# Two chained cross-attention layers on one core: every third late layer-1 step multiplies fp32 probabilities as they are, and one unit's heads are scaled in three blocks

## What is computed

```
text, ip = ctx[:, :77], ctx[:, 77:]          # 77 and 947 tokens
q, k, v      = heads(x @ Wq.T), heads(text @ Wk.T),    heads(text @ Wv.T)
k_ip, v_ip   = heads(ip @ Wk_ip.T), heads(ip @ Wv_ip.T)
out_text = softmax(q k^T / 4) v              # 20 heads, over 77 tokens
out_ip   = softmax(q k_ip^T / 4) v_ip        # over 947 tokens
x = x + (out_text + out_ip) @ Wo.T + bo
```

## Time and profile before

| | us |
|---|---|
| runs | 3522.02, 3520.13, 3520.0 |
| median | 3520.13 |
| span of the profiled execution, first to last instruction | 3517.6 |
| TensorE busy in it | 3406.7 (97%) |
| VectorE, ScalarE, GpSimd busy | 2044.4, 1845.3, 1095.2 |

### The profile page before, as it was taken

The page is one execution under the profiler, slowest core; times in us unless marked ns, Lnnn a source line. Parts: engine busy times, 40 slices in busy tenths (PEclk is TensorE's granted clock), DMA queues, the critical chain, the costliest instruction groups (busy, mean ns, idle before and its releaser), DMA issues.

```text
span 3517.6 us, 65886 instructions
## 1 busy us (share of the span) xinstructions
PE 3406.7 (97%) x24832; PEld 2900.3 (82%) x24832; DVE 2044.4 (58%) x5565; ACT 1845.3 (52%) x4030; POOL 1095.2 (31%) x932
## 2 busy tenths in 40 slices
PE   6999999999999999999999999999999999999978
PEld 4888978887888888888888878888788888889755
DVE  4444445556555565665656556656566656565678
ACT  2333333556454555555655555555555556565757
POOL 2111010234332332233333232333423322222467
PEclk8999999999999999999999999999999999999989
DMA  5433822233348333233356423324335532222233
GB/s 183 107 77 64 104 82 74 70 88 83 82 83 76 93 75 83 76 100 84 94 76 71 97 71 76 80 74 107 86 74 78 69 61 62 55 55 53 52 78 64
DMA packets 659087, 282.78 MB, mean 80 GB/s; under 512 B 481010, under 2 KB 609730, under 8 KB 658772
## 3 DMA queue, kind: packets, MB, share of 16 engines
q1 hardware_dynamic: 658772, 278.57, 38.2%
HBM read 199.44 MB, written 79.04 MB: 79 GB/s over the span
## 4 chain that ended last, share of the span: by engine, by line
PE 88%; DVE 6%; ACT 2%; issue 1%; POOL 1%; SPq 1%; DMA 1%; POOLq 0%; DVEq 0%; ACTq 0%
PE acc L1095 9%; PE acc L1088 9%; PE acc L1090 8%; PE acc L1091 8%; PE acc L1096 8%; PE acc L1089 7%; PE score L1055 4%; PE score L1139 4%; PE spare L1139 4%; PE score L1057 3%; PE av L1126 3%; PE av L1130 3%; PE score L1176 2%; PE spare L1176 2%; PE score L1225 2%; PE spare L1225 2%
## 5 line engine op out<-in xcount | busy, mean ns | idle before, releaser
L1298 ACT ACTIVATE prob<-score 128x512 f32<-128x512 f32 x1219 | 729.3, 598 | 1252.5 <-PE score L1057 1244.4
L1698 POOL TENSOR_TENSOR prob_lo<-prob,prob_hi 128x512 fp32r<-128x512 f32 x624 | 816.1, 1312 | 1525.5 <-ACT prob_hi L1301 1524.9
L1088 PE MATMUL acc<-tok_v,prob_hi 128*128 128x300 f32 x2240 | 904.1, 404 | 0.9 <-issue 0.9
L1090 PE MATMUL acc<-tok_lo,prob_hi 128*128 128x256 f32 (+1 forms) x2560 | 755.5, 295 | 0.0
L1095 PE MATMUL acc<-tok_v,prob_lo 128*128 128x278 f32 (+1 forms) x2560 | 745.8, 291 | 0.0
L1301 ACT ACTIVATE prob_hi<-score 128x512 fp32r<-128x512 f32 x1219 | 726.0, 596 | 0.0
L1091 PE MATMUL acc<-tok_lo,prob_hi 128*128 128x256 f32 (+1 forms) x2560 | 719.5, 281 | 0.0
L1096 PE MATMUL acc<-tok_v,prob_lo 128*128 128x256 f32 (+1 forms) x2560 | 717.7, 280 | 0.0
L1089 PE MATMUL acc<-tok_v,prob_hi 128*128 128x256 f32 x2240 | 627.4, 280 | 0.0
L1090 PEld LDWEIGHTS acc<-tok_lo,prob_hi 128*128 128x128 f32 (+1 forms) x2560 | 484.2, 189 | 9.1 <-issue 7.2
L1091 PEld LDWEIGHTS acc<-tok_lo,prob_hi 128*128 128x128 f32 (+1 forms) x2560 | 483.6, 189 | 6.3 <-issue 1.0
(11 more groups left out here) (325 smaller groups left out, 5141.1 us busy)
## 6 DMA issues: line engine op xcount, KB each, us to landing
k_ring<-k_scr SPq DMA_DIRECT2D x160, 384.0 KB
tok_v<-v_scr SPq DMA_DIRECT2D x158, 176.0 KB, 3.3
v_ring<-v_scr SPq DMA_DIRECT2D x160, 148.5 KB, 3.4
ctx_t<-in_ctxT SPq DMA_DIRECT2D x16, 1024.0 KB, 9.1
q_ring<-q_scr SPq DMA_DIRECT2D x160, 96.0 KB
v_scr<-v_stage SPq DMA_DIRECT2D x32, 440.0 KB, 2.6
v_scr<-v_stage SPq DMA_DIRECT2D x36, 330.0 KB, 9.6
tok_stage<-in_ctx SPq DMA_DIRECT2D x32, 256.0 KB, 2.9
```

The costliest lines, as they stand in the source:

```text
L1088: e.matmul(out_a[:, 0:SEG + VCOLS], p_hi, tok_v[0:kk, c, seg, v_lo:v_lo + SEG + VCOLS], start=first, stop=False)
L1090: e.matmul(out_a[:, t0:t0 + SEG], p_hi, tok_lo[0:kk, c, seg * SEG:(seg + 1) * SEG], start=False, stop=False)
L1298: e.activation(prob[:, es, :], bank_s[:, :], ACT.Exp, scale=SCALE)
L1698: e.tensor_tensor(prob_lo[:, ps, :], prob[:, es, :], prob_hi.bitcast(F32)[:, ps, :], ALU.subtract).then_inc(s_low[1], 1)
```

## The change

1. In the tail every third step is *whole* (`whole`, WHOLE_EVERY = 3: steps 1, 4, 7, ... of the 125). A whole step has one exp, into `prob`, no subtraction, and two products of `v_ring`, read as plain fp32, with `prob` itself. Its exp makes the next use of its slot wait for its products instead of for its subtraction.
2. The other tail steps have their subtraction on GpSimd, all of them.
3. The heads of unit 14 are scaled in three blocks of 8, 8 and 4, both parts in place in `heads_out`, each block when its heads are there; after the last, two sums (`combine_sum`) of text and image halves write `attn`.

```diff
+BY_BLOCKS = (LAST - 1, LAST)
+WHOLE_EVERY = 3
...
+        if u in BY_BLOCKS:
+            put_off(*[("combine_block", u, NM - 1, i) for i in range(3)], *[("combine_sum", u, st) for st in range(ST)])
+        else:
+            put_off(*[("combine", u, i) for i in range(3 if layer == 0 else 7)])
...
+        if u in BY_BLOCKS and h + 1 in [end for _, end in BLOCKS[:-1]]:
+            m = [end for _, end in BLOCKS].index(h + 1)
+            if u == LAST:
+                urgent.append((n + 5, lambda: last_block(m)))
+            else:
+                urgent.append((n + 5, lambda: put_off(*[("combine_block", u, m, i) for i in range(3)])))
...
-    on_pool = [layer_of[n] == 1 and (n < tail or n % 8 != 4) for n in range(len(chunks))]
+    on_pool = [layer_of[n] == 1 for n in range(len(chunks))]
+    whole = [n >= tail and (n - tail) % WHOLE_EVERY == 1 for n in range(len(chunks))]
...
@@ TensorE, av1
+                    if whole[n]:
+                        for k in range(UNIT_KEYS):
+                            mm = e.matmul(both[0:n_out[k], 0:SQ], weights[k].bitcast(F32), prob[:, n % E_SLOTS, queries[k]],
+                                          start=r == 0 and k == 0, stop=r == 0 and k == 0 or r == NU - 1 and k == 1,
+                                          skip_group_check=r > 0 or k > 0)
+                        mm.then_inc(s_main, 1)
+                        continue
...
@@ ScalarE, score
-                        e.wait_ge(s_low[on_pool[m]], low_nth[m])
+                        if whole[m]:
+                            e.wait_ge(s_main, m + 1)
+                        else:
+                            e.wait_ge(s_low[on_pool[m]], low_nth[m])
+                    if whole[n]:
+                        e.activation(prob[:, es, :], bank_s[:, :], ACT.Exp, scale=SCALE).then_inc(s_exp, 1)
+                        continue
...
@@ VectorE, combine_block piece 1, and combine_sum
-                        e.tensor_tensor(at, ho[:, :, :, 0:DH], wide[0], ALU.mult).then_inc(s_comb, 1)
+                        text = ho[:, :, :, 0:DH]
+                        e.tensor_tensor(at if u == LAST else text, text, wide[0], ALU.mult).then_inc(s_comb, 1)
...
+                elif kind == "combine_sum":
+                    _, u, st = s
+                    ho = heads_out[1][:, st, :, :]
+                    e.wait_ge(s_comb, comb_base[u, NM - 1] + 4)
+                    e.tensor_tensor(attn[:, st, :, :], ho[:, :, 0:DH], ho[:, :, DH:2 * DH], ALU.add).then_inc(s_comb, 1)
```

More of the change, by code:

```diff
@@ L508, in unit_done @@
             return
-        put_off(*[("combine", u, i) for i in range(3 if layer == 0 else 7)])
+        if u in BY_BLOCKS:
+            put_off(*[("combine_block", u, NM - 1, i) for i in range(3)], *[("combine_sum", u, st) for st in range(ST)])
+        else:
+            put_off(*[("combine", u, i) for i in range(3 if layer == 0 else 7)])
         if layer == 0:
@@ L600, in rows_of @@
         urgent.append((n + 3, lambda: turn_head(u, h)))
-        if u == LAST and h + 1 in [end for _, end in BLOCKS[:-1]]:
-            urgent.append((n + 5, lambda: last_block([end for _, end in BLOCKS].index(h + 1))))
+        if u in BY_BLOCKS and h + 1 in [end for _, end in BLOCKS[:-1]]:
[4 more added lines that the diff above has]
+                urgent.append((n + 5, lambda: put_off(*[("combine_block", u, m, i) for i in range(3)])))
         if h == HEADS - 1:
@@ L739, in cross_attention_pair @@
     layer_of = [UNITS[u][0] for _, u, _, _ in chunks]
-    on_pool = [layer_of[n] == 1 and (n < tail or n % 8 != 4) for n in range(len(chunks))]
+    on_pool = [layer_of[n] == 1 for n in range(len(chunks))]
+    whole = [n >= tail and (n - tail) % WHOLE_EVERY == 1 for n in range(len(chunks))]
     low_nth, seen = [], [0, 0]
     for n in range(len(chunks)):
-        seen[on_pool[n]] += 1
+        seen[on_pool[n]] += not whole[n]
         low_nth.append(seen[on_pool[n]])
@@ L921, in cross_attention_pair @@
         close0 = {s[1]: i for i, s in enumerate([s for s in o.steps if s[0] == "fuse_root"])}
-        comb_base, comb_here, base = {}, {}, 0
+        comb_base, comb_done, comb_here, base = {}, {}, {}, 0
         for s in o.steps:
@@ L929, in cross_attention_pair @@
             elif s[0] == "combine_block":
-                comb_base.setdefault(s[1], base)
+                comb_base.setdefault(s[1:3], base)
                 base += 2 if s[3] == 0 else 1
+                comb_done[s[1:3]] = base
+            elif s[0] == "combine_sum":
+                base += 1
+                comb_done[s[1], NM - 1] = base
         ip_nth = {s[1]: i for i, s in enumerate([s for s in o.steps if s[0] == "ip_norm"])}
@@ L1249, in _ @@
                     if k == 0:
-                        e.wait_ge(s_comb, comb_base[u] + (5 * (m + 1) if u == LAST else COMBINED[layer]))
+                        e.wait_ge(s_comb, comb_done[u, m if u == LAST else NM - 1] if u in BY_BLOCKS else comb_base[u] + COMBINED[layer])
                         if layer == 0:
@@ L1398, in _ @@
                     n = s[1]
-                    if not on_pool[n]:
+                    if not on_pool[n] and not whole[n]:
                         ps, es = n % P_SLOTS, n % E_SLOTS
@@ L1595, in _ @@
                     h0, h1 = BLOCKS[m]
-                    i0 = comb_base[u] + 5 * m
+                    i0 = comb_base[u, m]
                     ho = heads_out[1][:, :, h0:h1, :]
@@ L1694, in _ @@
                     n = s[1]
-                    if on_pool[n]:
+                    if on_pool[n] and not whole[n]:
                         ps, es = n % P_SLOTS, n % E_SLOTS
@@ L1875, in _ @@
                     w, nth_close = MW[m], close_nth[u]
-                    e.wait_ge(s_comb, comb_base[u] + (5 if u == LAST else COMBINED[layer]))
+                    e.wait_ge(s_comb, comb_done[u, 0 if u == LAST else NM - 1] if u in BY_BLOCKS else comb_base[u] + COMBINED[layer])
                     if nth_close:
```

## The result

The changed kernel takes 3509.51 us (median of 8 runs, 3506.83 to 3514.22) against 3520.07 us for the kernel before (8 runs, 3516.76 to 3525.22): a ratio of 0.9969, 95% interval 0.9959 to 0.9979. That is 10.6 us less, 0.31%, where 7.1 us less was forecast; the range of the prediction holds it, and of its three cases (faster by over 0.2%, within, slower) the first came. The profiled execution took 3506.83 us; it is the fastest of the eight.

A forecast was written before the change was run, and what follows sets the result against it. In 3440 to 3479 us GpSimd was taken as longest, with little between it and the other engines. By stretch, -4.2, -0.6 and -2.3 sum to -7.1 us against the median of 3520.13: 3513.0 us, range 3504 to 3524.

The forecast's parts named there:

- the price: Each whole step: two plain fp32 products instead of four fp32r ones cost TensorE +0.395 us at full clock.
- the blocks: Unit 14's heads, scaled earlier in three blocks, leave less VectorE work at its end: -3.0 us, gain of 1.3 to 4.5.
- three signs of being wrong: Exps waiting over some 3 us on products, fp32 products above 0.9 us a step, or TensorE's gap after unit 14 unchanged.
- The gap: TensorE's wait after unit 14's last head was to be 1 to 3.7 us instead of 5.17.
- 3308 to 3430 us, -4.2: First stretch, 65 steps, 22 whole: TensorE's cost +6.0, subtraction waits -3.3, less VectorE work -3.9, unit 14's heads -3.0 us.
- VectorE's relief: 3308 to 3430 us: VectorE loses 8 subtractions, 7.8 us, counted at half: -3.9 us (0 to -7.8).
- The waits on subtractions, -3.3: 3308 to 3430 us: of 4.3 us of such waits a third vanish and the others shrink (0 to -4.3).
- 3430 to 3490 us, -0.6: 48 steps, 16 whole: TensorE's cost +6.3, waits going -6.0 and -1.9, new slot wait +1.0 us (-3 to +4).
- From 3490 us, -2.3: Last twelve steps, four whole: ScalarE saves 1.9 us, GpSimd no longer behind, but the last step is whole (-4 to 0).
- The half clock does not come: Rival: with a shorter gap after unit 14 TensorE keeps 2.4 GHz, about 5 us more won: 3508; chance 0.20.
- The wash: Rival: stalls in 3308 to 3430 us are chains, so less VectorE work gains nothing: 3518.4 us; chance 0.22.
- The slot wait decides: Rival: ScalarE's exp after a whole step comes too late, leaving holes of 0.2 us or more: 3525.4 to 3533.8; chance 0.13.

The follow-up runs named there:

- e4: The changed kernel with 66 columns of v_ring instead of 33 in each whole-step product (values land in wrong output rows): 3509.04 us, ratio 0.9953 to the kernel before.
- e1: The kernel before with only unit 14's heads in three blocks, no whole steps, one subtraction of eight on VectorE: 3522.15 us, ratio 0.9996.
- phase 0: The changed kernel with steps 0, 3, ... 123 whole instead of 1, 4, ... 124: 3505.95 us, ratio 0.9949 to the kernel before; repeated, 3507.01 us.

## Why the prediction was right

It put the forecast just on the bound (0.45 faster, 0.48 no difference), and the time fell 3.5 us on the fast side of it. The mechanisms were those named, but of the sizes only some were right, and that the sum came so near is in part luck: the price was too small and the blocks probably worth less than put down, which made the forecast too good, and the rest of the first stretch was worth more, which made up for it. Two of its own three signs of being wrong came true: exps waited 14.3 us on products, not 3, and the fp32 products of a whole step cost 0.47 + 0.607 = 1.08 us, not under 0.9. The first did no harm, and the second cost what e4 gives back. The gap, at 0.89 us, shrank even below the 1 to 3.7 us named.

**The price** (+0.395 us a whole step at full clock). Too small by a third of the true one: +0.607. The prediction's upper case, +0.61, has the same number by luck: it came from products as dear as those of 320 columns, and they start 0.216 us apart as scaled. Scaling the columns of the earlier trace rows gave the spacing of plain fp32 products, 0.216 us, as it was measured, but the hole in front of and behind them isn't in rows 5 and 6, because there the neighbours have the same 128 columns of weights. Over 42 steps it is 8.9 us of TensorE's time at full clock; closing it gave 4.0 us of the tail, 5.6 by the ratios.

**3308 to 3430 us, -4.2.** Measured -7.2 in the first profile and -4.9 in the second, so how much is missing, 3.0 us or 0.7, is not known. The blocks alone gave 2.2 in this stretch where I took 3.0 in a range of 1.3 to 4.5, with a time that can't be told from no change. VectorE's relief was counted at half of its busy time, 0.49 us for each subtraction; undoing it costs 0.41 to 0.62 for each of 10 by the profiles and 0.56 by the ratios. So half was about right on average, and wrong as a picture: nine cost 0.2 to 0.5 us each, and one that began just after GpSimd's lasted 1.8 us ahead of maxima on which TensorE waits, and cost 2.1 us by itself. The waits on subtractions, -3.3, nearly vanished as forecast: the longest waits of TensorE's weight loads that are left are for the issue of their own engine and for maxima.

The forecast weighed a rule of the Trainium skill, page SBUF — State Buffer, section Who interferes with whom, by which a VectorE instruction with two SBUF inputs waits for the whole of a GpSimd instruction that reads SBUF and has begun before it. The profile had no four-head block beside a subtraction, and I took 0.29 us for it. The runs show 1.22, 1.28 and 0.70 us behind one, each ending 0.15 us after the subtraction, and 0.28 us where the block began first: the trace agrees with the rule. By that rule the sum was to be 1.7 us worse; the blocks alone were worth 0.8 less than my term in this stretch, a difference within what two profiles differ by. The gap shrank by 2.2 us in e1, more than the 1.3 of the rule's lower end.

**3430 to 3490 us, -0.6.** Measured -0.5. Right, though its terms were not. TensorE's price was 16 x 0.212 = 3.4 us higher than put down, and the waits that went were worth more: with them in it, a step from its second score product to what stands behind its products took 0.711 us on average before (32 steps from 3440 to 3479 us), 0.578 in the change's split steps. Over 32 steps that is 22.8 us before against 11 x 1.184 + 21 x 0.578 = 25.2 after, so within these products 2.4 us are lost net, and the rest of the steps gives them back. In 50 to 14 steps before the end the change is even 1.2 us slower than before: TensorE has become the bound there, as the part on what would show it had it. The prediction's own reading, that GpSimd was the longest in 3440 to 3479 us before, went by the waits; its row had ScalarE busier (38.68 of 39 us), and no run separates the two.

**From 3490 us, -2.3.** Measured -3.2, within its bounds of -4 to 0; no run takes it apart.

**The rivals.** *The half clock does not come* was partly true: the tail has 42.9 us at half clock before and 22.0 after, and in the ten steps behind unit 14 about 13.9 and 3.5. A gap of 0.89 us didn't fully prevent it, and with whole steps alone a gap of 3.1 us still left a mean of 0.85. I had priced this at up to 5 us besides the forecast; it may be the home of what is missing in the first stretch, but no run separates it from VectorE's relief. *The wash* fell with the relief. *The slot wait decides* fell at a period of three: ScalarE waits 14.3 us, and TensorE's weight loads wait 0.2 us for ScalarE meanwhile; what it does with every sixth step whole stays open.

## What to carry to other kernels

An engine at 75% that answers short questions of a full one can delay it by more than an instruction's own length: ask which of its long instructions stand ahead of an answer, and take their length beside the other engines and not their median. One of ten subtractions made 2.1 us here, the other nine 0.2 to 0.5 us each. When a product's form changes, its price is the time from the instruction before it to the one behind it, which a row of equal neighbours doesn't hold. Where a full engine must wait in any case, extra work on it costs little: place the dearer step there. And where a table of every third step meets a single event, such as a unit's end, try all phases: by the ratios the best is 3 to 7 us ahead of the two others, over a quarter of the whole gain. Last, take a second profile before explaining a difference of 2 us: two of one kernel differ by as much.

## What the runs showed of the hardware

- Plain fp32 products with 33 columns of weights that stand next to a product of another width leave holes on TensorE: the first starts 0.092 us late, the neighbour behind the last 0.096 us late, and between a 66- and a 33-column product there are 0.307 us instead of 0.216. With 66 columns throughout (e4) none of it is left, and the fp32r products of 33 columns in split steps show none (0.578 us for four of them and their neighbour). I had not expected narrower weights to be dearer.
- A VectorE multiplication on 128 x 128 took 0.28 us where it began ahead of GpSimd's subtraction, and 1.22 or 1.28 us where it began just after one of 1.27 us, ending 0.15 us behind it; a subtraction of VectorE's own took 1.78 us instead of 0.976.
- Ten steps with the same work took 16.7 us at a granted clock of 1.00 (phase 0) and 19.7 and 21.0 at 0.91 and 0.84 (the change, twice). The longer of TensorE's two gaps there was 0.88 us in the first and 1.48 or 1.49 in the others.
